# Second attention of a two-layer model: the place of ScalarE's copies, the engine of two subtractions, and the order of the query chunks

## The reference, cut to what matters

```
q        = rmsnorm(h @ wq_a.T) @ wq_b.T          # per head: 128 "nope" + 64 "rope" features
q_abs    = q_nope @ w_k[head]                    # 64 latent features
q_pe     = rope(q_pe)                            # rotated by cos and sin of the position
scores   = (q_abs @ kv.T + q_pe @ k_pe.T) * SCALE, causal mask
attn     = softmax(scores)
x        = (attn @ kv) @ w_v[head];  out = x @ wo.T
```

## Time and profile before

| what | value |
|---|---|
| median of three runs | 1639.2 us |
| the profiled execution | 1637.82 us, its span 1636.2 us |
| PE busy (x instructions) | 1300.0 us, 79% of the span |
| DVE, ACT, POOL busy | 904.1, 740.1, 501.5 us |
| mean granted TensorE clock | 0.909 of full speed |
| second attention, batch 0: first score matmul, last value matmul begins | 769.80 us, 1105.70 us |
| second attention, batch 1: first score matmul | 1254.45 us |

### The profile page before, as it was taken

One profiled execution on the slowest core, in us unless ns is written; L12 is line 12 of the kernel. 1 busy time (PEld: TensorE's weight loads), 2 busy tenths in 40 slices (PEclk: granted clock), 3 DMA queues, 4 the chain that ended last, 5 costly groups with the idle time before them and its releaser, 6 DMA issues. The chain is left out here.

```text
span 1636.2 us, 24271 instructions
## 1 busy us (share of the span) xinstructions
PE 1300.0 (79%) x7940; PEld 940.3 (57%) x7940; DVE 904.1 (55%) x2104; ACT 740.1 (45%) x1668; POOL 501.5 (31%) x488
## 2 busy tenths in 40 slices
PE   2666729999899839585899999997485999999977
PEld 2565615555555427474666666666474666666656
DVE  6646548777677243244666666650244666666640
ACT  1534404666565602433555555540334555555530
POOL 0222243333230000140555555520131554445520
PEclk9887959999999959787999999998797999999998
DMA  2312186555550096202100111005102001010005
GB/s 77 132 52 106 68 87 57 62 61 67 56 61 22 21 274 183 55 13 73 38 29 27 36 36 37 27 14 159 43 26 81 24 27 46 27 45 27 14 26 154
DMA packets 133170, 101.19 MB, mean 62 GB/s; under 512 B 48240, under 2 KB 120368, under 8 KB 132784
## 3 DMA queue, kind: packets, MB, share of 16 engines
q1 hardware_dynamic: 132000, 98.53, 26.8%
q10 hardware_dynamic: 1040, 1.05, 0.2%
HBM read 56.30 MB, written 34.87 MB: 56 GB/s over the span
## 5 line engine op out<-in xcount | busy, mean ns | idle before, releaser
L753 POOL TENSOR_SCALAR a_p<-a_p,a_rl 128x128 f32<-128x128 f32 (+7 forms) x256 | 215.6, 842 | 438.7 <-DVE a_rl L695 438.5
L736 ACT ACTIVATE a_p<-psum,a_nm 128x128 f32<-128x128 f32 (+7 forms) x256 | 190.2, 743 | 193.0 <-DVE a_nm L689 191.9
L1137 DVE TENSOR_REDUCE a_nmp<-psum 128x1 f32<-128x512 f32 (+3 forms) x384 | 198.9, 554 | 75.2 <-PE psum L1051 66.2
L1197 ACT ACTIVATE a_pt<-psum 128x512 f32<-128x512 f32 (+3 forms) x384 | 178.8, 490 | 130.5 <-PE psum L1066 95.5
L786 PE MATMUL psum<-ident,a_p 128*128 128x128 f32 x1152 | 187.5, 281 | 56.2 <-ACT a_pt L720 35.2
L1048 PE MATMUL psum<-a_op_k,a_op_q 128*128 128x512 f32 (+3 forms) x384 | 156.2, 417 | 40.1 <-DVE a_op_k L1186 33.0
L786 PEld LDWEIGHTS psum<-ident,a_p 128*128 128x128 f32 x1152 | 131.9, 142 | 94.4 <-ACT a_pt L720 52.1
L808 PE MATMUL psum<-a_pt,v 128*64 128x256 f32 (+1 forms) x1280 | 160.5, 373 | 2.0 <-ACT a_pt L720 2.0
L1063 PE MATMUL psum<-a_op_q,a_op_k 128*128 128x512 f32 (+3 forms) x384 | 156.9, 419 | 3.0 <-issue 2.6
L689 DVE CUSTOM_DVE_ANT_0 psum<-psum,mask_a 128x128 f32<-128x128 f32 (+3 forms) x128 | 63.7, 498 | 172.7 <-PE psum L771 172.6
L722 DVE COPY a_pt<-psum 128x512 f32<-128x512 f32 (+1 forms) x192 | 113.6, 591 | 11.9 <-PE psum L786 10.3
(11 more groups left out here) (266 smaller groups left out, 2835.0 us busy)
## 6 DMA issues: line engine op xcount, KB each, us to landing
a_swap<-a_raw SPq DMA_DIRECT2D x64, 128.0 KB, 2.3
ot_d<-a_ot SPq DMA_DIRECT2D x16, 512.0 KB, 2.6
o_ot<-ot_d SPq DMA_DIRECT2D x16, 512.0 KB, 6.4
a_raw_q<-qk_d SPq DMA_DIRECT2D x48, 128.0 KB, 5.5
a_raw_k<-qk_d SPq DMA_DIRECT2D x48, 128.0 KB, 9.4
a_wf<-wf_d SPq DMA_DIRECT2D x16, 384.0 KB, 3.4
qk_d<-p_stage_h SPq DMA_DIRECT2D x8, 512.0 KB, 2.7
qk_d<-p_stage_l SPq DMA_DIRECT2D x8, 512.0 KB, 3.4
```

The source lines that it names most:

```text
L736: e.activation(s.p[:, t % NPB, 0:(i + 1) * P], C.score[t % 2][:, 0:(i + 1) * P], ACT.Exp, scale=-1.0, bias=s.nm[:, k:k + 1], accum_out=s.l ...
L753: e.tensor_scalar(s.p[:, t % NPB, 0:(i + 1) * P], s.p[:, t % NPB, 0:(i + 1) * P], s.rl[:, k:k + 1], 1.0, ALU.mult, ALU.mult).then_inc(s.no ...
L1137: e.tensor_reduce(nmp[c][:, hd, i % 4, w:w + 1], a_banks[k % 3][:, 0:n], AX.X, ALU.max, negate=True).then_inc(a_maxed[k % 3], 1)
L1197: e.activation(pt[:, k // G0 % NPT, hd, off:HALF], b_banks[k % 3][:, off:HALF], ACT.Exp).then_inc(exped, 1)
```

## The change

Three edits of the second attention, made together, and the tables that go with them.

1. ACT's slot t copies out the odd units of step t-4 instead of t-5, ahead of the exponential of step t. DVE's copies stay at t-5.
2. The low parts of the rotated rows go from DVE to POOL, in slots 13 and 14, after that slot's scaling, each followed by a wait for its own end. They count on a semaphore of their own, `qrest`.
3. The chunks come in the order 3, 0, 2, 1, and the preparation tables shift by two slots: PE and ACT's first four pieces to slots 2, 4, 6, 8; DVE's latent low parts to 7 and 9; POOL's rotations to 6 to 11. ACT's last two high parts stay in slots 12 and 13.

```diff
-        self.steps = [(c, hd, 2 * c + i) for c in range(NQC) for hd in range(heads) for i in range(2)]
+        self.order = (3, 0, 2, 1)
+        self.steps = [(k, hd, 2 * c + i) for k, c in enumerate(self.order) for hd in range(heads) for i in range(2)]
...
 def evacuate(e, C, s, n, t, later, parity):
-    tt = t - LAG - 1
+    tt = t - LAG - (1 - parity)
...
-        n_k = 2 * c + 2
+        n_k = 2 * core.order[c] + 2
...
+        def rest_pool(e, g, u, hd, done):
+
+            r = PE_ROWS[hd]
+            e.wait_ge(qhi, g * 6 + 5 + hd)
+            e.wait_ge(s.normed, done)
+            e.tensor_tensor(q[u][hd][1][r, :], raw[r, :], q[u][hd][0][r, :].bitcast(F32),
+                            ALU.subtract).then_inc(qrest, 1)
+            e.wait_ge(qrest, g * 2 + hd + 1)
...
-        AT_PE = {0: 0, 2: 1, 4: 2, 6: 3}
-        AT_ACT = {0: 0, 2: 1, 4: 2, 6: 3, 12: 4, 13: 5}
-        AT_DVE = {5: 2, 7: 3, 13: 4, 14: 5}
-        AT_POOL = {4: 0, 5: 1, 6: 2, 7: 3, 8: 4, 9: 5}
+        AT_PE = {2: 0, 4: 1, 6: 2, 8: 3}
+        AT_ACT = {2: 0, 4: 1, 6: 2, 8: 3, 12: 4, 13: 5}
+        AT_DVE = {7: 2, 9: 3}
+        AT_REST = {13: 0, 14: 1}
+        AT_POOL = {6: 0, 7: 1, 8: 2, 9: 3, 10: 4, 11: 5}
...
                     if t < core.SI and t % PREP == 0:
                         g = t // PREP
                         e.wait_ge(qhi, (n * 2 + g + 1) * 6)
-                        e.wait_ge(qlo, (n * 2 + g + 1) * 6)
+                        e.wait_ge(qlo, (n * 2 + g + 1) * 4)
+                        e.wait_ge(qrest, (n * 2 + g + 1) * 2)
...
-                    return ot[:, g % 2, c * QC:(c + 1) * QC]
+                    return ot[:, g % 2, core.order[c] * QC:(core.order[c] + 1) * QC]
...
+                    nxt = next_pair(n, t, last, AT_REST)
+                    if nxt:
+                        rest_pool(e, *nxt, n * core.SI + t + 1)
```

More of the change, by code:

```diff
@@ L1703, in attend1 @@
         qlo = ph.sem("qlo")
+        qrest = ph.sem("qrest")
         PE_ROWS = (slice(64, 128), slice(0, 64))
@@ L1717, in prep_pe @@
                 if later:
-                    e.wait_ge(qlo, g * 6)
+                    e.wait_ge(qlo, g * 4)
             elif not later:
@@ L1724, in prep_pe @@
                 e.wait_ge(qhi, g * 6 + 2)
-                e.wait_ge(qlo, g * 6 + 2)
+                e.wait_ge(qlo, g * 4 + 2)
             c = k % 2
@@ L1741, in prep_act @@
                     e.wait_ge(qhi, g * 6)
-                    e.wait_ge(qlo, g * 6)
+                    e.wait_ge(qrest, g * 2)
                 t = slice(k * HALF, (k + 1) * HALF)
@@ L1770, in prep_dve @@
                 e.tensor_tensor(q[u][hd][1][r, :], raw[r, :], q[u][hd][0][r, :].bitcast(F32),
-                                ALU.subtract).then_inc(qlo, 1)
+                                ALU.subtract).then_inc(qrest, 1)
[4 more added lines that the diff above has]
+            e.tensor_tensor(q[u][hd][1][r, :], raw[r, :], q[u][hd][0][r, :].bitcast(F32),
+                            ALU.subtract).then_inc(qrest, 1)
+            e.wait_ge(qrest, g * 2 + hd + 1)
         def rotate(e, g, k):
```

## The result

The changed kernel takes 1715.26 us in the median of 4 runs (1707.99 to 1716.58) against 1638.28 us before: ratio 1.0464, 95% interval 1.0433 to 1.0496, slower. The forecast was 1720 us, its range 1658 to 1762.

A forecast was written before the change was run, and what follows sets the result against it. PE was taken to set the pace, busy 39.3 of 43 us. Middle groups of 32.85 + 14.1 + 1.75 = 48.7 us, with first and last groups, add 81 us to 1639.2: 1720 us, range 1658 to 1762.

The forecast's parts named there:

- The chain of slots 10 to 15: Late preparation through POOL, ACT and DVE: PE's slots 12 to 15 take 14.1 us for 6.2 us of work.
- The sign named for it: Profile sign of being right: a POOL subtraction in slots 13 and 14 takes 2.4 to 2.7 us.
- The other twelve slots: PE's slots 0 to 11 of a middle group: 32.85 us, plus 1.75 us for a slow clock.
- The slow clock: After 5.3 us idle at each group's end PE runs some 3.5 us at half speed, costing 1.75 us a group.
- The base of 42.65 us: Period of one group before the change, averaged over six groups taking 255.9 us.
- The 6.2 us of work in slots 12 to 15: PE's work in the light last four slots: scores 2.7 us, transposes 2.5 us, and values of chunk 0.
- The sum: Middle group 48.7 us, 72.6 us more over 12; first groups +19.5, last -11.1; in all +81 us.
- DVE's waits: PE's waits for DVE's copies, 8.3 us in seven groups, all credited as gone because the subtractions leave DVE.
- The order: Chunk order 3, 0, 2, 1: PE's work stays the same; shifted load, exchange and store cost nothing.
- cheap and dear subtraction: POOL's subtraction at 1.2 to 1.9 us: 1658 to 1682 us, chance 0.12; at 4.0 us: 1761 us, chance 0.06.
- the hidden ones: POOL's subtraction hidden, rotations not: 1625 to 1650 us, chance 0.07; both hidden, PE the bound: 1581 us, chance 0.09.

The follow-up runs named there:

- rests_dve: The changed kernel with the two rotated low parts back on DVE in slots 13 and 14; 1665.08 us, ratio 1.0173.
- new_order_pool_early: The changed kernel with earlier preparation: rotations in slots 3 to 8, ACT's rotated high parts in 9 and 10, POOL's subtractions in 10 and 11; 1622.42 us.
- copies_ahead: The kernel before with edit 1 alone, ACT's odd copies of step t-4 ahead of the exponential; 1601.31 us, ratio 0.9781.
- order_alone: The kernel before with the chunk order 3, 0, 2, 1 alone, all tables as before; 1658.96 us, ratio 1.0148.
- early_rests_dve: The changed kernel with the preparation tables of the kernel before and the subtractions on DVE in slots 13 and 14; 1638.39 us, ratio 1.0018.
- double_rest: The changed kernel with each of POOL's two subtractions done twice; 1787.81 us, ratio 1.093.
- pool_rests_alone: The kernel before with edit 2 alone, the two rotated low parts on POOL in slots 13 and 14; 1713.60 us, ratio 1.0489.

## Why the prediction was right

- **The chain of slots 10 to 15**: forecast 14.1 us, measured 14.2. ACT's high part was put 5.0 us after PE's slot 12 begins, and came at 901.97 - 897.17 = 4.8. The subtraction was priced 2.55 and took 2.34 us, but each is followed by its own wait, 0.23 us, and preceded by one of 0.15 us for the scaling, which the forecast left out; that these errors cancel is luck. The sign named for it, 2.4 to 2.7 us, was just missed.
- **The other twelve slots**: 32.85 + 1.75 = 34.6 us forecast, 33.8 measured. The slow clock had 1.75 us of it. Slots 0 to 3 take 12.9 us on average and 11.34 in the second and third group of `rests_dve`, which has no 5 us of idleness ahead of them and a granted clock of 1.00 in them, so about 1.6 us by that comparison. The base of 42.65 us was too high: it averages in two groups of 43.4 and 43.6 us, whose slots 0 to 3 ran at a granted clock of 0.88, where the others took 42.2. The 6.2 us of work in slots 12 to 15 were too low: in `new_order_pool_early` they took 7.84 us, of which PE waited 0.87 and 0.10, so about 6.9.
- **The sum**: middle group 48.7 forecast, 48.09 on average over six. The twelve middle groups cost 67.7 us more than before against 72.6, a first group 11.1 us against 9.75, and a last one gave 7.3 and 7.0 back against 5.55. That makes 75.7 us in the groups; some 2 us more lie outside them. Batch 0 began its last value matmul 37.6 us later (1146.47 against 1108.89 us; the 1105.70 us of the table ahead is where the last unbroken run of them begins), batch 1 78 us later; the forecast was 81. The mechanism is the one forecast, but that the total came within 3 us owes something to errors of both signs.
- **Edit 1** was priced as a gain, and it is one (36 us alone). That it would cost nothing held nearly: the changed kernel has no listed wait of PE for an exponential, and `copies_ahead` has nine, 1.6 us in seven groups.
- **DVE's waits**: I credited all 25.2 us of rows 2. Seven of DVE's waits are left in the changed kernel, 9.3 us (1.32 us each in slot 8, where the latent subtraction of slot 7 is in front of a copy). That term was too good by about 1.3 us a group. The base and the work of slots 12 to 15, wrong the other way by 0.4 and 0.7 us, hid most of it in the sum; about 1 us of the twelve slots is not accounted for.
- **The order** was priced at nothing by itself, and the loss put on the preparation. `order_alone` says 23 us without edit 1, and `early_rests_dve` against `copies_ahead` 37 us with it. In the changed kernel the chain of slots 12 to 15, which the forecast did price, covers part of this, but as a separate statement it was wrong: with the subtractions on DVE the order loses in slots 4 to 8 as well as at the group's light end.
- **The rivals**: cheap and dear subtraction fell with 2.34 us; the hidden ones fell with `double_rest` and the wait of 5 us.

## What to carry to other kernels

Work that must be ready at a loop's turn is to be costed from the slot at which its engine really gets there (here POOL's slot 14 began at 908.06 us, a microsecond after the last transpose of PE's slot 15), not from the number of the slot. An engine that is 31% busy can still be the bound for a tenth of the time, and beside edit 1 moving the subtractions to it cost 82 us in slots 13 and 14 (1601.31 to 1683.15 us) and nothing that shows in slots 11 and 12 (1596.76 us). An order of steps that gives one engine a light stretch gains nothing there if the others have a full load in it.

## What the runs showed that I had not expected

The three edits don't add up: alone they give -36, +77 and +23 us (the order without its shifted tables, which were not run alone), 64 in sum, and together +77. Added one after the other they give -36 us (edit 1, 1601.31 us), +37 (the order, 1638.39), +27 (the shifted tables, 1665.08) and +50 (the subtractions on POOL, 1715.26): so 64 of the 114 us that the change loses against edit 1 alone are there without the subtractions on POOL. Edit 1 is worth 36 us in the old order with DVE's subtractions and 30 with POOL's; in the new order it is worth 21 us with DVE's and the old tables, and 77 with POOL's and the shifted ones.

POOL's scaling of 896 columns took 1420 ns on average before and 1014 ns after. One that began at 880.91 us, beside DVE's subtraction of two SBUF inputs, had taken 1.94 us. With that subtraction off DVE the mean fell to that of an undisturbed one, also in `pool_rests_alone`, in the old order: 1016 ns. In `rests_dve` it is the scaling of 512 columns that meets DVE's subtraction, 1031 ns on average for 695 before. The Trainium skill's SBUF — State Buffer (Who interferes with whom) says that a DVE instruction with two SBUF inputs and a GpSimd instruction that reads SBUF exclude each other on a shared port; the trace agrees, 1.94 against 1.01 us. What this was worth to PE no run shows apart from the rest.
